# A state-space and expert kernel: full-height dt product, square before logarithm, nine products of the first batch on VectorE

## The reference

```python
xn = _layernorm(x)
xz = einsum('ed,bld->bel', in_proj_w, xn)            # x and z, 256 channels each
# for each of two directions (forward, and reversed in time):
u = silu(causal_conv(x, w, 4 taps) + b)
x_dbl = einsum('bdl,kd->bkl', u, xproj_w)            # 8 rows for dt, 16 for B, 16 for C
delta = softplus(einsum('dr,brl->bdl', dtproj_w, x_dbl[:, :8]) + dt_bias)
h = scan(exp(delta * A), delta * B * u)              # over time, 256 channels x 16 states
y = (sum over n of h * C + D * u) * silu(z)
mamba = einsum('bdl,od->blo', y_f + y_b, out_proj_w)
# experts: for each row the 4 best of 16, by -|x - key|^2 + x.rw + rb, softmax of the four
ffn = sum of w * (gelu(x @ w1 + b1) @ w2 + b2)
```

## Time and profile before

| | |
|---|---|
| median of three runs | 1164.04 us (1156.34 to 1166.79) |
| profiled execution | 1173.3 us, span 1170.8 |
| mean granted clock of PE | 0.926 |
| DVE busy | 1067.2 us, 91% of the span |
| PE, ACT, POOL busy | 948.1, 909.4, 889.6 us |
| DMA | 222.61 MB, mean 190 GB/s |

### The profile page before, as it was taken

The page is one execution under the profiler, slowest core; times in us unless marked ns, Lnnn a source line. Parts: engine busy times, 40 slices in busy tenths (PEclk is TensorE's granted clock), DMA queues, the critical chain, the costliest instruction groups (busy, mean ns, idle before and its releaser), DMA issues.

```text
span 1170.8 us, 21578 instructions
## 1 busy us (share of the span) xinstructions
PE 948.1 (81%) x5764; PEld 743.6 (64%) x5764; DVE 1067.2 (91%) x1392; ACT 909.4 (78%) x1647; POOL 889.6 (76%) x540
## 2 busy tenths in 40 slices
PE   5358878863789998888898888988989998897972
PEld 5223333322678777777787777777768777786862
DVE  7896888858999999999999989999999999997992
ACT  2038787776799988888898878889889988987920
POOL 1077868774469997997989798889979997997642
PEclk9967878775899999999999999999999999998995
DMA  9924444558656776686777666767866776665555
GB/s 311 344 77 163 177 161 181 221 214 295 199 166 169 219 190 182 180 231 180 181 207 195 176 167 187 190 190 178 230 174 182 207 206 174 172 163 155 135 120 155
DMA packets 151296, 222.61 MB, mean 190 GB/s; under 512 B 36028, under 2 KB 97756, under 8 KB 146276
## 3 DMA queue, kind: packets, MB, share of 16 engines
q1 hardware_dynamic: 124036, 202.16, 54.4%
q0 software_dynamic: 27136, 19.02, 11.7%
HBM read 159.74 MB, written 65.52 MB: 192 GB/s over the span
## 4 chain that ended last, share of the span: by engine, by line
issue 21%; POOL 13%; DMA 8%; DVE 5%; ACT 5%; PE 4%; SPq 1%; DVEq 1%; POOLq 0%; ACTq 0%
POOL arena L750 7%; POOL acc_d L735 6%; DMA acc_d<-yrows,tags 6%; DVE arena L1392 3%; DVE ps L1380 2%; ACT arena L936 2%; PE ps L1114 1%; DMA tags<-slots_d 1%; PE ps L1085 1%; ACT arena L876 1%; ACT arena L904 1%; ACT arena L857 1%; DMA arena<-acc_d 0%; PE ps L1106 0%; ACT yrows L882 0%
## 5 line engine op out<-in xcount | busy, mean ns | idle before, releaser
L1392 DVE TENSOR_TENSOR_SCAN arena<-arena,ps 128x512 f32<-128x512 f32 x512 | 599.5, 1200 | 2.4 <-issue 2.4
L750 POOL TENSOR_TENSOR arena<-arena 128x1024 f32<-128x1024 f32 x237 | 510.1, 2439 | 96.0 <-DVE arena L1392 84.9
L936 ACT ACTIVATE arena<-delta,a_neg 128x511 f32<-128x511 f32 x512 | 338.5, 725 | 8.3 <-DVE arena L1392 4.9
L735 POOL DMA_INDIRECT acc_d<-yrows,tags x160 | 251.8, 1574 | 62.2 <-issue 36.4
L1085 PE MATMUL ps<-ident,arena 128*128 128x128 f32 x2048 | 272.5, 277 | 3.5 <-DVE arena L1400 3.5
L1380 DVE TENSOR_TENSOR ps<-du,ps 128x512 f32<-128x512 f32 x384 | 252.8, 672 | 15.4 <-PE ps L1149 13.2
L1085 PEld LDWEIGHTS ps<-ident,arena 128*128 128x128 f32 x2048 | 235.2, 143 | 15.9 <-DVE arena L1400 4.0
L717 POOL DMA_INDIRECT slots_d<-arena,pos x128 | 155.6, 1216 | 42.1 <-issue 40.6
L1114 PE MATMUL ps<-w,arena 128*128 128x128 f32 x1248 | 175.3, 284 | 1.4 <-issue 0.9
L1106 PE MATMUL ps<-rowsT,w 128*128 128x256 f32 x640 | 155.1, 386 | 9.5 <-ACT arena L887 7.1
L1114 PEld LDWEIGHTS ps<-w,arena 128*128 128x128 f32 x1248 | 154.0, 193 | 10.8 <-issue 2.4
(11 more groups left out here) (142 smaller groups left out, 938.7 us busy)
## 6 DMA issues: line engine op xcount, KB each, us to landing
arena<-c_d SPq DMA_DIRECT2D x128, 512.0 KB
w<-w_dram SPq DMA_DIRECT2D x80, 258.0 KB
w<-w_dram SPq DMA_DIRECT2D x80, 256.0 KB
rows<-slots_d SPq DMA_DIRECT2D x80, 130.0 KB
slots_d<-delta SPq DMA_DIRECT2D x5, 2015.0 KB, 19.9
delta_d<-arena SPq DMA_DIRECT2D x8, 1024.0 KB
du_d<-delta SPq DMA_DIRECT2D x8, 1024.0 KB
delta<-delta_d SPq DMA_DIRECT2D x8, 1024.0 KB, 6.8
```

Source lines behind the costliest of these rows:

```text
L735: pool.indirect_dma_start(acc_d, bass.IndirectOffsetOnAxis(ap=tags[:, j, a, 0:1].bitcast(I32), axis=0), yrows[:, j % W_RING, a, :], None, ...
L750: nc.gpsimd.tensor_tensor(state[:, q % H_RING], state[:, q % H_RING], c_rows[:, r % C_RING], ALU.mult).then_inc(s["prod_done"], 1)
L936: nc.scalar.activation(decay[:, q % DA_RING, j, lo:lo + L - 1], delta[:, par, dh, lo:lo + L - 1], ACT.Exp, scale=a_neg[:, dh, 2 * g + j:2 ...
L1392: nc.vector.tensor_tensor_scan(state[:, q % H_RING, j, way], decay[:, q % DA_RING, j, way], b_ps[:, ROW[q, j], j, way], 0.0, ALU.mult, ALU ...
```

## The change

- The dt product runs over all 128 rows. Before, its operands were rows 96 to 104 of `dtw` and `xdbl`. Now the whole tile `dtw` is zeroed by POOL first, SP waits for that (`dtw_zeroed`) before it loads the weights, and ACT waits for `ones_ready` before its first copy into `xdbl`.
- On ACT, the square stands ahead of the logarithm. On DVE, in batches 1 to 6, the last tap of the next batch's convolution stands behind `small`.
- `FIRST_VECTOR` is 0 to 8: DVE makes the first nine products with C of the first batch.
- `FIRST_T` is [8, 10, 11, 13, 14] in place of [5, 7, 9, 11, 13] for its first five tiles, and `FIRST_U` follows by one step for these.
- POOL sets `ones`, and PE multiplies it by itself 80 times at the start. The two `drop` operations of DVE stand before the router's logits.

```diff
-FIRST_VECTOR = (1, 4, 7)
+FIRST_VECTOR = tuple(range(9))
-FIRST_T = [5, 7, 9, 11, 13] + T_STEP[GROUP:]
-FIRST_U = [q + 2 for q in FIRST_T]
+FIRST_T = [8, 10, 11, 13, 14] + T_STEP[GROUP:]
+FIRST_U = [q + (1 if q < T_STEP[GROUP] else 2) for q in FIRST_T]
+WARM = 80
...
+            sp.wait_ge(s["dtw_zeroed"], 1)
             for dst, src in ((chan[:, :, :], chan_in), (inw, inw_in), (xproj, xproj_in), (dtw[BR:BR + NR], dtw_in),
...
+            nc.gpsimd.memset(ones[:, :], 1.0).then_inc(s["ones_set"], 1)
+            nc.gpsimd.memset(dtw, 0.0).then_inc(s["dtw_zeroed"], 1)
             nc.gpsimd.memset(delta[:, :, :, :], 0.0).then_inc(s["zero_v"], 1)
...
-                act.wait_ge(s["exp_ready"], b + 1)
                 wait(act, s["sum_ready"], ND * b)
-                nc.scalar.activation(ln1p, mag, ACT.Ln, scale=LN_SCALE, bias=ln_bias[:, 0:1]).then_inc(s["ln_ready"], 1)
                 act.wait_ge(s["small_ready"], b + 1)
                 nc.scalar.activation(fit, small, ACT.Square, scale=SQ_SCALE, bias=fit_bias[:, 0:1]).then_inc(s["square_ready"], 1)
+                act.wait_ge(s["exp_ready"], b + 1)
+                nc.scalar.activation(ln1p, mag, ACT.Ln, scale=LN_SCALE, bias=ln_bias[:, 0:1]).then_inc(s["ln_ready"], 1)
...
+            pe.wait_ge(s["ones_set"], 1)
+            for k in range(WARM):
+                nc.tensor.matmul(ps[:, 0, 0:P], ones[:, :], ones[:, :], start=True, stop=True)
...
-                        last = nc.tensor.matmul(ps[:, DT_BANK + d * NH + h, :], dtw[BR:BR + NR + 1, d, h * P:(h + 1) * P],
-                                                xdbl[BR:BR + NR + 1, d, :], start=True, stop=True)
+                        last = nc.tensor.matmul(ps[:, DT_BANK + d * NH + h, :], dtw[:, d, h * P:(h + 1) * P], xdbl[:, d, :],
+                                                start=True, stop=True)
...
-                    convolve(b + 1)
+                    convolve(b + 1, range(KC) if b == 0 else range(KC - 1))
...
                 nc.vector.tensor_scalar(small, mag, SMALL, None, ALU.min).then_inc(s["small_ready"], 1)
+                if 0 < b < BATCH - 1:
+                    convolve(b + 1, range(KC - 1, KC))
```

More of the change, by code:

```diff
@@ L436, in build_kernel @@
             late_in1 skip_in0 skip_in1 decay_ready b_ready dbx_done scan_done prod_done v_prod_done summed y_free m0_ready m0_free m1_ready m1_free gelu_done
-            b2_in b2_split b2_out turn_ps turned scaled
+            ones_set dtw_zeroed ones_ready b2_in b2_split b2_out turn_ps turned scaled
             mixed_out mixed_in sp_step pool_step acc_ready out_done"""
@@ L802, in prepare @@
                 wait(act, s["c_out"], 16 * b)
+                if b == 0:
+                    act.wait_ge(s["ones_ready"], 1)
                 for d in range(ND):
@@ L1186, in _ @@
             nc.vector.memset(ones_b, 1.0)
-            nc.vector.memset(ones[:, :], 1.0)
             nc.vector.memset(fit_bias[:, :], SQ_BIAS)
@@ L1223, in _ @@
             link(nc.vector.tensor_tensor(route_b, rb, ps[:, 6, 0:E], ALU.subtract))
+            for k in range(2):
+                last = nc.vector.tensor_scalar(drop[0:BR, k, :], consts[0:BR, C_ID:C_ID + BR], consts[0:BR, C_PART + k:C_PART + k + 1],
+                                               None, ALU.mult)
+            last.then_inc(s["drop_ready"], 1)
             dve.wait_ge(s["logit_ps"], 1)
@@ L1276, in _, with convolve @@
             nc.vector.tensor_scalar(a_neg[:, :, :], a_neg[:, :, :], -1.0, None, ALU.mult)
[L1278 to L1282, removed]
+            def convolve(b, taps):
+                if taps[0] == 0:
+                    dve.wait_ge(s["xpad_ready"], b + 1)
+                    wait(dve, s["u_ready"], ND * b)
+                for k in taps:
                     for q in range(DH):
@@ L1345, in _ @@
             start = done[0]
-            convolve(0)
+            convolve(0, range(KC))
             nc.vector.memset(parts_p[BR:P], 0.0)
[L1348 to L1352, removed]
+            nc.vector.memset(xdbl[BR:P], 1.0).then_inc(s["ones_ready"], 1)
             for b in range(BATCH):
```

## The result

The changed kernel takes 1177.74 us (median of four runs, 1175.03 to 1186.87); the kernel before took 1164.47 beside it (1156.34 to 1166.79). The ratio is 1.0117, 95% interval 1.0079 to 1.0154. Forecast was 1159, with a range up to 1170. The change makes the kernel about 1% slower, and the time lies outside the range.

A forecast was written before the change was run, and what follows sets the result against it. Scans were taken as bound by DVE, preparation by the ring ACT to PE to ACT. 14.5 - 5.1 - 2.5 - 2.0 = 4.9 us saved, 1164.0 to 1159; own range 1154 to 1164, eight in ten 1150 to 1170.

The forecast's parts named there:

- the last scatter: First batch: last scatter unchanged at 272.0, so product 8's C row, needed near 301, is hidden with over 10 us to spare.
- hold-ups: Nine DVE products beside GpSimd scatters: none held up, 0 taken; if each were, 1.7 us more each, 15 in all.
- Preparation: Preparation of the eight batches: 12.0 + 0.6 + 1.9 = 14.5 us saved, ending at 260.9 instead of 275.4.
- the order in the last batch: Square ahead of logarithm in the last batch of preparation: L1313 starts earlier, and preparation ends 1.9 us earlier.
- Batch 0: Batch 0 of the preparation: only a wait of about 0.6 us there, which goes.
- The last interval: Preparation, 239.45 to 262.20: L1031 already ran at full clock, so nothing saved.
- Nine products: First batch of scans: products 0 to 8 on DVE, not 1, 4, 7, cost 5.1 us more.
- The wait for C: First batch: product 0 on DVE waits for the rows of C, a new cost of 2.5 us.
- Dense tiles: First five expert tiles in steps 8 to 15: 2.0 us of DVE idle, between 0 and 8.
- Start: Start: 80 PE products do not change the router's clock, 0 taken; up to 5 us lost if they ended at 19.
- Rival B: Start stays fast: router's products end near 28.3, not 34.0, 5.7 us more saved, 1153; chance 0.13.
- Rival D: First scans starve: ACT or PE falls behind in steps 8 to 19, 8 instead of 2, 1165, up to 1170; chance 0.16.

The follow-up runs named there:

- e4_gaps: The changed kernel with six one-column DVE memsets per batch, one ahead of each two-input softplus operation behind the taps; 1165.9 us, ratio 0.9985.
- g1_one_gap: The changed kernel with one one-column DVE memset per batch, ahead of the first L1329 only; 1164.9 us, ratio 0.9971.
- f1_dt128: The kernel before with only the dt product over all 128 rows (with its zeroing and two waits); 1162.8 us, ratio 0.9966.
- e5_nine_rows: e4_gaps with the dt product put back over 9 rows; 1175.9 us, ratio 1.0084.
- e7_four: e4_gaps with four products with C of the first batch on DVE, not nine; 1160.4 us, ratio 0.9948.
- f2_spread: e7_four with products 0 and 1 moved to product 2's place and the first five tiles at their old steps; 1157.5 us, ratio 0.9936.
- e6_no_warm: e4_gaps without the 80 small PE products at the start; 1163.8 us, ratio 0.9983.

## Why the prediction was wrong

**The step that failed** is the one on the last scatter: "these wait for the last scatter, issued at 272.0 and unchanged", with product 8 "hidden, with over 10 us to spare". It was issued at 296.99, DVE stood 9.33 us for product 8's rows of C where 10 were to spare, and 17.4 us of idle time came together where 4.5 (2.5 and 2.0) were forecast. Behind it is a second sentence, on hold-ups: "I take none, since DVE's two-input operations beside scatters in the preparation keep their 1.2". That was read from DVE's side only. DVE did keep its 1.2 (2.35 for two, 117.84); the scatter beside it paid. Before, the bound and 3.50 us of idle time stood between the taps and L1313; the moved tap took both away. The prediction counted that wait as slack of DVE alone, and weighed no row of POOL but the last.

The Trainium skill (SBUF — State Buffer, section "SBUF: two separate sides") says that VectorE's operations with two inputs in SBUF and GpSimd's instructions that read SBUF contend for a shared pair of ports under an exclusive lock, held for a whole instruction. The held scatters agree with a lock. By one operation's length a scatter would take at most 1.2 us more, 2.2 in all (an estimate from that rule and the durations of the rows), and up to 2.0 is what e4_gaps and g1_one_gap show; the 4.6 and 8.9 us more in the changed kernel and in f1_dt128 are several instructions long, and there the measurement decides.

**Preparation**, 14.5 forecast: 15.6 measured. The terms held: clock (3.60 for 5.81), the 1.48 of wait gone, 21.3 to 21.8 us in five batches (21.8 forecast). The six intervals together save 12.1 (12.0 forecast), and the order in the last batch 1.9. Two smaller terms were off. Batch 0 saves 2.2 and not 0.6: its skip product, 5.29 us before, had run at the low clock too. The last interval takes 0.6 more than before, where nothing was forecast. In it and in the batch ahead of it the projection behind a pause cost more than the 0 to 0.9 allowed for: `project_u` (L1018) took 6.59 and 6.02 us, and 3.66 at full clock (e4_gaps). e5_nine_rows ties the gain to the rows (12.4 us).

**Nine products**, 5.1: 5.7 measured in DVE's busy time, and 5.7 for five of them in e7_four.

**The wait for C**, 2.5: 4.48, and 4.2 in e4_gaps. The mechanism was right, and DVE was there 5.5 us after the end of the preparation (265.33 less 259.83) as forecast; the rows of C took 10.0 from there and not 8.1.

**Dense tiles**, 2.0: not seen apart from the late rows. In e4_gaps two waits for PE, of 1.31 and 0.41; f2_spread shows no difference between dense and spread.

**Start**, 0: confirmed (e6_no_warm). Rival B had no ground.

With the scatters on time (e4_gaps) the second batch starts 2.7 us earlier than before, and the time is the same within its interval: the forecast gain of 4.9 us (a ratio of 0.996) lies at the edge of that interval, 0.9958 to 1.0013. Rival D had the right effect, starving in the first batch, but its cause was ACT or PE and its price 8; here it was a DMA queue, and 17.4.

**What stays open.** The trace puts 7.4 us of the change's loss ahead of the second batch. The medians differ by 13.3, and by about 10.5 if before is taken at the 1167 of the later comparisons. The rest isn't located: the profiled executions are single ones, and that of before (1173.3) lay 9 us above its median. In these two the stretch from the second batch on took 790 us before and 785 after, so no trace here shows a loss behind it. Why going from the taps straight into L1329 holds a scatter over several instructions, and a memset of one column ends that, is not settled either, nor why f1_dt128 held one scatter beside taps that held none in the kernel before.

## What to carry to other kernels

When an edit takes a wait away from VectorE, look at what GpSimd did in that wait, and read GpSimd's rows in both kernels before calling its stream unchanged. A queue entry that waits for "all done" is a lever: 25 us on the last scatter moved tiles, rows of C and the products behind them, and neither order of the queue could save both. And a shorter stage is worth only what the next stage can start with: here 15 us of preparation were worth 2.7 at the second batch with the scatters on time, and 8.9 when GpSimd had five of the products back.

## What the runs showed of the hardware

- A GpSimd indirect DMA instruction of 1.0 us took 4.9 to 5.6 us, and a later one 2.96, in each batch in which VectorE's operations with two f32 inputs in SBUF followed the taps without a break (the changed kernel); one took 9.95 beside the taps themselves (f1_dt128). They ended 0.82 to 0.84 us after an operation of VectorE. VectorE's own durations in the preparation didn't change (2.35 and 2.36 for two).
- One VectorE memset of 128x1 (0.06 us in the trace, nothing measurable in the time) at the join let scatters in at the ends of single operations for the rest of the run; none took over 2.01 us (g1_one_gap).
- With a TensorE product over 9 rows the granted clock fell from 1.00 to 0.50 in a busy stretch in most batches: the skip product behind it ran slow in five of eight in e5_nine_rows and in seven of eight in the kernel before. Over 128 rows, with the same columns, it ran slow in none of the eight batches of twelve traces.
- 80 small products at the start (7.15 us in the changed kernel, then 4.21 without work for TensorE) left the 64 weight loads of the router at 0.333 us, as without them.
